# Ranks masked ahead of the scores' maximum, and row scatters that signal three semaphores in turn and wait for the third one ahead

## The reference, cut to what matters

```python
# third step: attention (keys and values are both the context)
scores = einsum('bsd,bmd->bsm', layernorm(x), ctx) * scale
scores = where(mask, scores, -1e30)
x = x + einsum('bsm,bmd->bsd', softmax(scores), ctx)
# fourth step: experts
h = layernorm(x)
weights, chosen = top_k(softmax(h @ gate_kernel), 8)      # 2048 tokens, 8 experts each
rows = h[token_rows sorted by expert]
y = down(silu(gate(rows)) * up(rows))                      # by expert
x = x + sum over the 8 of weight * y
```

## Time and profile before

| what | value |
|---|---|
| three runs | 1464.87 us median (1462.42 to 1499.52) |
| the profiled execution | 1463.59 us, of which the span is 1461.8 us |
| TensorE clock granted, mean of the span | 0.982 |
| PE busy | 1368.3 us, 94% of the span |
| DVE busy | 967.4 us, 66% |
| POOL busy | 383.7 us, 26% |

### The profile page before, as it was taken

One profiled execution on the slowest core, in us unless ns is written; L12 is line 12 of the kernel. 1 busy time (PEld: TensorE's weight loads), 2 busy tenths in 40 slices (PEclk: granted clock), 3 DMA queues, 4 the chain that ended last, 5 costly groups with the idle time before them and its releaser, 6 DMA issues.

```text
span 1461.8 us, 27798 instructions
## 1 busy us (share of the span) xinstructions
PE 1368.3 (94%) x7685; PEld 743.8 (51%) x7686; DVE 967.4 (66%) x2434; ACT 578.0 (40%) x1075; POOL 383.7 (26%) x313
## 2 busy tenths in 40 slices
PE   4799999999999999999998649999999999999996
PEld 2344444444444444454544326666666666666663
DVE  7979757975895646687776536555655565556654
ACT  0444443444334443432222114444444444444442
POOL 1000000000000000015655553344343444444443
PEclk9999999999999999999999869999999999999998
DMA  9976776767777678737767778999999999989886
GB/s 372 381 288 203 259 264 225 251 202 237 229 238 221 234 266 300 271 129 260 252 237 282 275 255 207 252 205 269 268 262 239 247 239 239 261 218 224 159 163 88
DMA packets 132698, 353.44 MB, mean 242 GB/s; under 512 B 15009, under 2 KB 15521, under 8 KB 125729
## 3 DMA queue, kind: packets, MB, share of 16 engines
q1 hardware_dynamic: 73488, 215.11, 43.6%
q0 software_dynamic: 34640, 85.74, 25.5%
q10 hardware_dynamic: 24512, 51.89, 10.8%
HBM read 196.87 MB, written 155.81 MB: 241 GB/s over the span
## 4 chain that ended last, share of the span: by engine, by line
PE 72%; DVE 14%; DMA 4%; issue 3%; ACT 2%; another core or an unknown queue 2%; SPq 1%; ACTq 1%; POOL 0%; POOLq 0%; DVEq 0%
PE PS L1715 19%; PE PS L1717 19%; PE PS L1716 19%; PE PS L1978 5%; PE PS L2012 2%; PE PS L2011 2%; PE PS L2001 2%; DMA split_experts<-HT 1%; DVE HT L1162 1%; DVE EX L1338 1%; DMA BIG<-in_wdT 1%; DVE EX L1344 1%; PE PS L1669 1%; DMA CST<-in_kv 1%
## 5 line engine op out<-in xcount | busy, mean ns | idle before, releaser
L607 POOL DMA_INDIRECT out<-BIG,EX x159 | 247.6, 1557 | 340.8 <-issue 169.3
L1715 PE MATMUL PS<-BIG 128*128 (+1 forms) x795 | 269.2, 339 | 11.5 <-DVE BIG L1608 11.5
L1716 PE MATMUL PS<-BIG 128*128 (+1 forms) x795 | 269.2, 339 | 0.0
L1717 PE MATMUL PS<-BIG 128*128 (+1 forms) x795 | 269.1, 339 | 0.0
L1715 PE MATMUL PS<-HT,BIG 128*128 128x512 f16 (+1 forms) x512 | 194.1, 379 | 4.5 <-DVE EX L1153 1.5
L1716 PE MATMUL PS<-HT,BIG 128*128 128x512 f16 (+1 forms) x512 | 194.0, 379 | 0.0
L1717 PE MATMUL PS<-HT,BIG 128*128 128x512 f16 (+1 forms) x512 | 194.0, 379 | 0.0
L579 POOL DMA_INDIRECT rows_by_expert<-HT,POS x128 | 124.5, 973 | 122.6 <-DVE POS L1429 87.6
L1613 DVE SCALAR_TENSOR_TENSOR BIG<-PS,BIG 128x192 f32<-128x192 f32 x159 | 56.6, 356 | 139.2 <-ACT BIG L840 110.6
L1717 PE MATMUL PS<-BIG,EX 128*128 128x512 f16 (+1 forms) x376 | 143.3, 381 | 1.0 <-issue 1.0
L1715 PE MATMUL PS<-BIG,EX 128*128 128x512 f16 (+1 forms) x376 | 143.0, 380 | 0.7 <-issue 0.4
(11 more groups left out here) (262 smaller groups left out, 2186.7 us busy)
## 6 DMA issues: line engine op xcount, KB each, us to landing
BIG<-rows_by_expert ACTq DMA_DIRECT2D x159, 280.0 KB
HT<-in_experts SPq DMA_DIRECT2D x64, 640.0 KB, 4.9
split_experts<-HT SPq DMA_DIRECT2D x128, 320.0 KB, 2.8
BIG<-split_experts SPq DMA_DIRECT2D x32, 1280.0 KB
CST<-in_kv SPq DMA_DIRECT2D x64, 256.0 KB, 4.9
split_context<-RT SPq DMA_DIRECT2D x64, 256.0 KB, 4.8
BIG<-split_context SPq DMA_DIRECT2D x7, 2048.0 KB
rows_by_expert<-X SPq DMA_DIRECT2D x32, 280.0 KB
```

The lines of the kernel that those rows point to most:

```text
L607: pool.indirect_dma_start(a_out, bass.IndirectOffsetOnAxis(ap=IDY[:, u % V:u % V + 1], axis=0), yt[u % V], None, compute_op=ALU.add).then_ ...
L1715: mm(out, lh, rh, start=first, stop=False)
L1716: mm(out, lh, rl, start=False, stop=False)
L1717: return mm(out, ll, rh, start=False, stop=last_group)
```

## The change

Three edits:

1. DVE's order in a step t > 0: the query tile's normalisation (L1111, `ROWS`) and the statistics of a later tile (L1049, L1051) move ahead of `scores_max(t + 1)`, and so does `place_first(t - 2)`. `place(t - 2)` stays behind it.
2. The scatters of tiles 0 to 12 signal three semaphores in turn (`QUEUED = 3`). Ahead of each scatter POOL waits until the scatter three before it has landed.
3. Who waited for a slot's semaphore (DVE before it overwrites a slot, ACT before the first load) now waits for all three.

```diff
+QUEUED = 3
-def scatters_of(tile):
-    return 16 * TOPK * (tile // ZN)
+def wait_scatters(eng, sems, tile):
+    last = tile * TOPK + TOPK - 1
+    for r in range(QUEUED):
+        index = last - (last - r) % QUEUED
+        eng.wait_ge(sems[r], 16 * (index // QUEUED + 1))
...
-        s_ids = [sem(f"rows_sorted{i}") for i in range(ZN)]
+        s_ids = [sem(f"rows_sorted{i}") for i in range(QUEUED)]
...
                 for w in columns:
                     c = TOPK - 1 - w
+                    index = t * TOPK + w
+                    if t < NT - 3:
+                        wait(pool, s_ids[index % QUEUED], 16 * (index // QUEUED))
                     pool.indirect_dma_start(d_row, bass.IndirectOffsetOnAxis(ap=POS[:, t % ZN, c:c + 1], axis=0),
-                                            ZR[:, t % ZN, :], None).then_inc(s_ids[t % ZN] if t < NT - 3 else s_add[w], 16)
+                                            ZR[:, t % ZN, :], None).then_inc(s_ids[index % QUEUED] if t < NT - 3 else s_add[w], 16)
...
-            for t in range(NT - ZN, NT - 3):
-                act.wait_ge(s_ids[t % ZN], scatters_of(t + ZN))
+            wait_scatters(act, s_ids, NT - 4)
...
                     if t - 1 >= ZN:
-                        dve.wait_ge(s_ids[(t - 1) % ZN], scatters_of(t - 1))
+                        wait_scatters(dve, s_ids, t - 1 - ZN)
                     dve.wait_ge(s_rcz, 1)
                     tile_normalise(ZR[:, (t - 1) % ZN, 0:D], t - 1, 0).then_inc(s_nr, 1)
...
+                if t and query:
+                    wait(dve, s_qt, t)
+                    tile_normalise(ROWS[:, (t + QA + 1) % 2, :], t + QA + 1, 1).then_inc(s_nq, 1)
+                if t and t + QA + 2 < NT:
+                    tile_stats(stats, 1, t + QA + 2)
+                    stats += 1
+                if t > 1:
+                    place_first(t - 2)
                 scores_max(t + 1)
                 if t > 1:
-                    place_first(t - 2)
                     place(t - 2)
-                if query:
-                    wait(dve, s_qt, t)
-                    tile_normalise(ROWS[:, (t + QA + 1) % 2, :], t + QA + 1, 1).then_inc(s_nq, 1)
...
             def last_normalise(n, tile):
-                dve.wait_ge(s_ids[tile % ZN], scatters_of(tile))
+                wait_scatters(dve, s_ids, tile - ZN)
```

More of the change, by code:

```diff
@@ L1461, in _ @@
                     dve.wait_ge(s_cst, 1 + 16 * 2 * NE)
+                if t and query:
[6 more added lines that the diff above has]
+                    place_first(t - 2)
                 scores_max(t + 1)
                 if t > 1:
-                    place_first(t - 2)
                     place(t - 2)
-                if query:
-                    wait(dve, s_qt, t)
-                    tile_normalise(ROWS[:, (t + QA + 1) % 2, :], t + QA + 1, 1).then_inc(s_nq, 1)
                 if t == 0:
+                    if query:
+                        tile_normalise(ROWS[:, (t + QA + 1) % 2, :], t + QA + 1, 1).then_inc(s_nq, 1)
                     dve.wait_ge(s_val, B)
@@ L1472, in _ @@
                     dve.wait_ge(s_val, B + 1)
-                if t + QA + 2 < NT:
                     tile_stats(stats, 1, t + QA + 2)
```

## The result

The changed kernel takes 1479.77 us (median of 1474.72 to 1483.57), the kernel before 1463.86 on the same chip: a ratio of 1.0113, 95% interval 1.0097 to 1.0129, some 16 us slower. The profiled execution took 1483.57 us, 20.0 more than the one of before.

What follows compares the result with a forecast made beforehand. It took the loop through POOL, 13.68 us a step, as the bound, not PE's 12.3. From 1463.59 us: +1.2 (order) + 0 (waits) + 0.2 = 1465 us, range 1448 to 1480 us.

Steps and rivals of the forecast that it cites:

- The loop of 1.70 + 0.45 + 8.95 + 2.58 us: Attention steps: maximum to places, to first scatter, to last scatter, to next maximum; 13.68 us, against PE's 12.3.
- Part 1: The new order on DVE: +0.1 us a step, +1.2 us in 12 steps, bounds 0 and +4 us.
- The 10.7 us buy nothing in the loop: PE's 10.7 us of waits for the masked ranks nearly go, but the loop through POOL gains nothing.
- Part 2: The waits ahead of POOL's scatters: 0 in quiet tiles, and 0 taken in loaded ones, bounds -1.4 and +3 us each.
- POOL's 3.75 us of rest: POOL's idle time in each step, claimed not to be spare because the signals' release follows the last scatter.
- One hold of 2.3 us: In a tile meeting SP's load, the seventh scatter waits over 2.3 us for the fourth; six or seven such tiles.
- The 0.2 us for the three-fold waits: DVE and ACT waiting for three semaphores: some 0.05 us for nine times, under 0.5 us, counted as 0.2.
- The quiet tiles: Tiles meeting no load: the scatter three ahead started 3.84 us earlier and has landed, so waits cost 0.
- POOL is held by landings: Rival: loaded tiles' holds go whole into the loop, +7 to +20 us, 1475 us; chance 0.19, beyond 1493 us 0.04.
- the cure: Rival: fewer scatters queued on POOL end the late signals, steps fall towards 12.32 us; 1450 us, chance 0.27.
- POOL's series run into each other: Sign of error: one tile's scatters on POOL following the previous tile's without separation.
- The distance of 2.58 us: From a tile's last scatter start to the next maximum's start; a change in quiet tiles would prove the forecast wrong.

Runs made afterwards that it cites:

- run 1: Only the change's DVE order, put into the kernel before, with its semaphores and scatters kept: 1464.04 us, ratio 1.0022.
- run 3: The changed kernel with seven semaphores, so each scatter waits for the seventh ahead instead of the third: 1464.82 us, ratio 0.9997.
- run 4: The kernel before, with the last two of a tile's eight scatters waiting for the next maximum in tiles 0 to 11: 1461.33 and 1463.62 us.
- run 2: Only the change's three semaphores and waits, put into the kernel before, with DVE's order kept: 1479.29 us, ratio 1.0102.
- Run 8: The changed kernel with two semaphores, so each scatter waits for the second ahead instead of the third: 1495.71 us, ratio 1.0223.
- run 14: The changed kernel, unaltered, on a chip where the kernel before takes 1433.00 us: 1450.03 us, ratio 1.0123.
- run 13: The kernel before itself, unaltered, traced on a chip of the faster sort: 1433.00 us.
- run 9: The kernel before, with POOL clearing 48 unused words twice ahead of the third, fifth and seventh scatter of tiles 0 to 12: 1432.72 us, ratio 0.9994.
- run 17: The kernel of run 9 again, against the kernel before, on a chip of 1463 us: ratio 0.9966.
- run 6: The changed DVE order in the kernel before, with each tile's last four scatters waiting for the next tile's low-half probabilities (tiles 0 to 11): 1463.82 us, ratio 1.0004.

## Why the prediction was wrong

**What bounds the kernel now: right for its chip, and not general.** The loop of 1.70 + 0.45 + 8.95 + 2.58 us is there on the chips of 1463 us (runs 1 and 3 have it too, run 4 with the series shifted). That signals are late while a series runs is borne out by the merged series and by run 4; that all of PE's and DVE's wait for its end is too strong, since within the series of 17 one of PE's came through and one of DVE's was in time. On the chips of 1433 us the same instructions make steps of 12.4 us. A trace of one chip couldn't show that.

**Part 1: right.** Forecast +1.2 us with bounds of 0 and +4; the run with the order alone has 1.0022 (0.9993 to 1.0052), some +3 us of -1 to +8, and its first load where it was. "The 10.7 us buy nothing in the loop" holds. PE's wait for the ranks didn't fall to near 0 in that run (7.3 us), though it did in the whole change (0.6 us).

**Part 2: the step that failed.** I wrote "I take 0, the middle", for a hold between -1.4 and +3 us a tile, and ahead of it that POOL's 3.75 us of rest "isn't spare, since the release follows the last scatter". The term that I put at 0 measured 16 us: run 2 has the waits alone and the whole loss, and seven ahead has none of it. Three things are wrong there. First, I priced a hold tile by tile, as if the series stayed apart. Held, POOL soon had two tiles' places at hand; the series of 13 and 17 scatters made two steps of 21.2 and 24.4 us, and tile 9's places came 16.1 us late. Second, I left out a path, POOL's own list: 128 scatters in a row of which the 114th lets the expert stage begin. On it the rest ahead of `POS` is spare while the places are in time, and holds cost what they exceed that rest by. In the change this path adds 3.8 us and keeps the 16.1 us from being made up. Run 8 shows it alone (last places 24 us earlier, end 34 us later), and so does run 14 (the loss without a late step). Third, the size. One hold of 2.3 us for each of six or seven loaded tiles is 14 to 16 us. There were 15 waits with 38.8 us, up to 6.4 us each: a landing under load takes up to 10.1 us (run 13), and with three in flight several scatters of one tile meet one, since after a hold the next three run on and then stand again. Whether holds of 14 to 16 us would have cost anything no run shows.

The 0.2 us for the three-fold waits of DVE and ACT rests on 0.05 us a wait, for which I had no row; seven-fold waits in run 3 cost nothing that its 0.9997 shows.

**The quiet tiles: right.** Seven ahead shows that waits that have passed cost nothing, and three ahead held none of tile 8's scatters (777.39 to 786.30), where nothing loaded. The scatters' time from issue to landing in the kernel before on the chip of run 13:

```profile
DMA to landing us min/median/max: 2.8/4.6/10.1
```

The estimate from the Trainium skill ("DMA: Bandwidth & Descriptors", "Anatomy of one DMA — SWDGE (gpsimd) path") of 2.66 us lies near the shortest of them only. By that page's figure no wait would have bound; the median and the maximum speak against using it under load.

**The rivals.** "POOL is held by landings", 1475 us with 0.19, was the right one, in both halves: the holds go into the loop (though as two long steps, not as 2 to 3 us for each loaded tile), and tiles 13 to 15 are late and the first load with them (though it waits for the first scatter of tile 15, not for "the last of them"). I had the mechanism, the condition (three scatters over 3.84 us to land) and the rows, and gave it less than the cure. What I set against it, that "with fewer scatters in flight SP's loads finish earlier", had no row. Its price of +7 to +20 us holds the 16 us measured; as the price was made of other parts, that is in part luck. The cure is seen in the steps (run 8, and the short steps of the change), and brought nothing in time, since POOL became the bound.

**The signs.** I named "POOL's series run into each other" as what would make me wrong, and they did. The distance of 2.58 us between last scatter and maximum is 2.8 and 3.0 us behind the plain series of eight that end at 695.59 and 786.30, and near 10 us behind the two long ones. The holds were expected near 728 and 783 ahead of a seventh scatter; they came at 659 to 744 and 797 to 843.

## What to carry to other kernels

A queue whose last needed item starts the next stage is a path of its own: add up its busy time and its rest from its first item to that item, and set a new wait against the rest as well as against the step of the loop beside it. Then look for the last place at which the queue stands for another engine: what is late there came from outside, and only what lies behind it is the queue's own. A wait "three ahead" was free here while a transfer took less than three issues (3.84 us), and under load a transfer took up to eight (10.1 us); seven ahead was free on the chip that ran it. The pauses of run 9 are the one version here that was nowhere slower than either kernel, on the three chips that ran it: 0.34% faster than before on a chip of 1463 us, and the same on those of 1433.

## What the runs showed of the hardware

The same kernel takes 1463 us on three chips and 1433 us on two. Of the 30.7 us between two traces of it, 22.6 lie ahead of the first load (850.55 and 827.95) and 8.1 behind it (611.3 and 603.2 us). On the slower chips PE's results reached the other engines late while GpSimd issued indirect DMAs 1.27 us apart, in the trace of the change up to 11.0 us after PE had finished. With 1.7 us or more after nearly every second one and at most two under way the steps were 12.3 us (run 8); with 1.59 us after every second one half of them were 13.2 us and most others longer (run 17), and with one pause of 0.9 us in eight they stayed at 13.8 us (run 6). What in those chips delays the signal no run here shows, nor whether the 8 us behind the first load, where GpSimd also issues indirect DMAs, have the same cause.
